# Gate/up product of a mixture-of-experts kernel with the weights as stationary operand, copied by ScalarE, in place of transposing the product's result

## The reference

```
x = x + attention(layernorm(x))              # 16 heads, 4 kv heads, window of 32
h = layernorm(x)                             # 8192 tokens
w, selected = sparsemixer(h @ router_w.T)    # two of 8 experts for each token
for e in range(8):
    g = silu(h @ w_gate[e].T) * (h @ w_up[e].T)      # 256 features
    out += dense_w[:, e:e+1] * (g @ w_down[e].T)
x = x + out
```

## Time and profile before

| | us |
|---|---|
| median of 3 runs | 601.63 |
| lowest, highest | 601.54, 603.01 |
| the profiled execution | 603.13 |
| its span, first to last instruction | 601.3 |
| PE, DVE, POOL, ACT busy in the span | 531.7, 446.0, 337.1, 332.9 |
| mean granted TensorE clock | 0.970 |

### The profile page before, as it was taken

One profiled execution on the slowest core, in us unless ns is written; L12 is line 12 of the kernel. 1 busy time (PEld: TensorE's weight loads), 2 busy tenths in 40 slices (PEclk: granted clock), 3 DMA queues, 4 the chain that ended last, 5 costly groups with the idle time before them and its releaser, 6 DMA issues. The chain is left out here.

```text
span 601.3 us, 20442 instructions
## 1 busy us (share of the span) xinstructions
PE 531.7 (88%) x6060; PEld 382.0 (64%) x6060; DVE 446.0 (74%) x1764; ACT 332.9 (55%) x1171; POOL 337.1 (56%) x468
## 2 busy tenths in 40 slices
PE   0599999899999999999984799999999999999970
PEld 0267787677777777777763466666666666666650
DVE  2569999999999999999999455646565555656553
ACT  1446776667767667767653455454544455444530
POOL 1222221866668766668754748264655655557655
PEclk9999999999999999999998599999999999999995
DMA  9512211332223322212231223244655554554543
GB/s 304 186 36 45 46 28 37 73 68 63 58 66 75 71 52 48 51 55 59 57 84 49 76 85 119 76 132 130 164 140 142 146 141 136 143 147 132 150 112 86
DMA packets 123530, 58.06 MB, mean 97 GB/s; under 512 B 53793, under 2 KB 118689, under 8 KB 123169
## 3 DMA queue, kind: packets, MB, share of 16 engines
q1 hardware_dynamic: 112640, 34.90, 23.6%
q0 software_dynamic: 8192, 16.79, 9.9%
q10 hardware_dynamic: 2592, 5.07, 2.2%
HBM read 28.14 MB, written 24.64 MB: 88 GB/s over the span
## 5 line engine op out<-in xcount | busy, mean ns | idle before, releaser
L1205 POOL DMA_INDIRECT expert_in<-xn,slot_r x128 | 127.5, 996 | 88.5 <-DVE slot_r L837 64.4
L1274 POOL DMA_INDIRECT ga<-expert_out,row_all x128 | 122.2, 954 | 92.4 <-DVE yb L1168 30.4
L653 PE MATMUL chb<-wgu,xbT 128*128 x288 | 151.1, 607 | 0.0
L1161 DVE TENSOR_TENSOR h<-sil,chb 128x256 f32<-128x256 f32 x144 | 60.6, 421 | 102.3 <-ACT sil L466 102.2
L381 ACT ACTIVATE pT<-chb 128x512 f32<-128x512 f32 x128 | 76.5, 598 | 83.6 <-DVE mx L854 49.2
L466 ACT ACTIVATE sil<-chb 128x256 f32<-128x256 f32 x144 | 55.4, 384 | 121.4 <-PE chb L653 121.4
L667 PEld LDWEIGHTS chb<-ident,h 128*128 128x128 f32 x288 | 40.5, 142 | 79.0 <-issue 42.5
L854 DVE TENSOR_REDUCE mx<-chb 128x8 f32<-128x512 f32 x128 | 85.4, 676 | 2.6 <-PE chb L577 2.1
L667 PE MATMUL chb<-ident,h 128*128 128x128 f32 x288 | 55.6, 275 | 1.5 <-DVE h L1161 1.4
L1229 POOL TENSOR_TENSOR tq<-t,rr 128x128 f32<-128x128 f32 x64 | 27.0, 421 | 48.7 <-issue 44.2
L596 PE MATMUL pp<-wp,xyT 128*128 128x272 f32 x128 | 50.2, 476 | 4.2 <-DVE t L939 2.6
(11 more groups left out here) (142 smaller groups left out, 1156.6 us busy)
## 6 DMA issues: line engine op xcount, KB each, us to landing
xb<-expert_in SPq DMA_DIRECT2D x144, 64.0 KB, 1.8
expert_out<-yb SPq DMA_DIRECT2D x72, 128.0 KB, 1.9
xa<-x SPq DMA_DIRECT2D x16, 256.0 KB, 3.1
out<-oo SPq DMA_DIRECT2D x32, 128.0 KB, 2.1
qk<-qk SPq DMA_DIRECT2D x64, 48.0 KB
wgu<-w_gu ACTq DMA_DIRECT2D x1, 2048.0 KB, 8.8
expert_in<-xn,slot_r POOLq DMA_INDIRECT x128
ga<-expert_out,row_all POOLq DMA_INDIRECT x128, 2.6
```

The costliest lines, as they stand in the source:

```text
L653: nc.tensor.matmul(chb[:, b % 2, :], xbT[:, b % 4, :], wgu[:, e, :], start=True, stop=True).then_inc(gu_done, 1)
L1161: nc.vector.tensor_tensor(h[:, b % 4, :], sil[:, b % 2, :], chb[:, b % 2, FF:2 * FF], ALU.mult).then_inc(h_ok, 1)
L1205: nc.gpsimd.indirect_dma_start(xs_dram, bass.IndirectOffsetOnAxis(ap=slot_r[:, q % 4, 2 * v + k:2 * v + k + 1], axis=0), xn2[:, t % 16, :] ...
L1274: nc.gpsimd.indirect_dma_start(ga[:, q % 2 * TPS + v, j, :], None, ys_dram[0:blocks * P, :], bass.IndirectOffsetOnAxis(ap=row_all[:, q * T ...
```

## The change

The product L653 is turned round: the weights become the stationary operand, in four pieces of 128 columns (two of gate, two of up), and xbT the moving one. The result then has the expert's features in partitions and tokens in columns, gate in the first half of a bank and up in the second. That is the layout the down product needs, and DVE writes hT itself. The stage B_HT goes, with PE's two transposes and ACT's copy of hT. Since the expert's number is only known in a register, ACT copies the expert's 512 gate and up columns to a fixed tile wcur (three buffers) in a stage of its own, B_COPY = 3, after the xbT copy of the slot; it reads the word and works out the expert itself, and waits that the product three blocks before has been done. chb is used in four banks instead of two and two. The down product stays at lag 7. PE needs the expert for that one only and reads its word at slot 5 of 8 instead of 3.

```diff
@@ -52,7 +52,7 @@
 (L_TY, L_XN2, L_TX2, L_RT, L_RANK, L_SCAT) = (14, 19, 20, 20, 23, 27)
 STEPS = NT + L_SCAT
 
-(B_LOAD, B_BT, B_GU, B_HT, B_DN, B_STORE) = (0, 3, 5, 6, 7, 8)
+(B_LOAD, B_COPY, B_BT, B_GU, B_DN, B_STORE) = (0, 3, 3, 5, 7, 8)
 C_FIRST = 5
 MEM = 8
 S_MOE = NT + L_PV
@@ -202,7 +202,8 @@
         summed = sb("summed", [1, NB // U])
 
         xb, xbT = sb("xb", [P, U, DIM]), sb("xbT", [P, 4, P])
-        sil, h, hT = sb("sil", [P, 2, FF]), sb("h", [P, 4, FF]), sb("hT", [P, 4, FF])
+        wcur = sb("wcur", [P, 3, 2 * FF])
+        sil, hT = sb("sil", [P, 2, FF]), sb("hT", [P, 4, FF])
         yb = sb("yb", [P, U, DIM])
         ga = sb("ga", [P, 8, 2, DIM])
         acc, oo = sb("acc", [P, 2, DIM]), sb("oo", [P, 4, DIM])
@@ -235,8 +236,8 @@
             "cols_ok", "colsT_done", "tabs_ok", "tail_ok", "tail_in"))
         xb_in = [sem(f"xb_in{n}") for n in range(U)]
         yb_out = [sem(f"yb_out{n}") for n in range(4)]
-        bt_done, xbT_ok, gu_done, sil_ok, h_ok = (sem(n) for n in ("bt_done", "xbT_ok", "gu_done", "sil_ok", "h_ok"))
-        ht_done, hT_ok, dn_done, yb_ok = sem("ht_done"), sem("hT_ok"), sem("dn_done"), sem("yb_ok")
+        bt_done, xbT_ok, wcur_ok, gu_done = sem("bt_done"), sem("xbT_ok"), sem("wcur_ok"), sem("gu_done")
+        sil_ok, hT_ok, dn_done, yb_ok = sem("sil_ok"), sem("hT_ok"), sem("dn_done"), sem("yb_ok")
         limits_ok, row_chain, comb_ok = sem("limits_ok"), sem("row_chain"), sem("comb_ok")
         gath = [sem(f"gathered{n}") for n in range(2 * TPS)]
         stored = [sem(f"stored{n}") for n in range(2)]
@@ -458,22 +459,31 @@
             for s in range(S_MOE):
                 step(s)
 
+            word = {}
+
             def slot(s):
                 b = block_at(s, B_GU)
                 if b is not None:
                     act.wait_ge(gu_done, b + 1)
-                    wait(act, h_ok, b - 1)
-                    nc.scalar.activation(sil[:, b % 2, :], chb[:, b % 2, 0:FF], ACT.Silu).then_inc(sil_ok, 1)
-                b = block_at(s, B_HT)
-                if b is not None:
-                    act.wait_ge(ht_done, b + 1)
-                    wait(act, dn_done, b - 3)
-                    nc.scalar.copy(hT[:, b % 4, :], chb[:, 2 + b % 2, 0:FF]).then_inc(hT_ok, 1)
+                    wait(act, hT_ok, b - 1)
+                    nc.scalar.activation(sil[:, b % 2, :], chb[:, b % 4, 0:FF], ACT.Silu).then_inc(sil_ok, 1)
                 b = block_at(s, B_BT)
                 if b is not None:
                     act.wait_ge(bt_done, b + 1)
                     wait(act, gu_done, b - 3)
                     nc.scalar.copy(xbT[:, b % 4, :], tp[:, 0:P]).then_inc(xbT_ok, 1)
+                b = block_at(s, B_COPY)
+                if b is not None:
+                    if b == 0:
+                        act.wait_ge(c_moe, 32)
+                        act.wait_ge(tabs_ok, 1)
+                    if b == NBA:
+                        act.wait_ge(tabs_ok, 2)
+                    if b % U == 0:
+                        word[b // U] = act.value_load(packed[0:1, b // U:b // U + 1], min_val=0, max_val=EXP ** U - 1)
+                    e = word[b // U] >> b % U * (EXP - 1).bit_length() & EXP - 1
+                    wait(act, gu_done, b - 2)
+                    nc.scalar.copy(wcur[:, b % 3, :], wgu[:, e, :]).then_inc(wcur_ok, 1)
 
             for s in range(NB + B_STORE):
                 d = drain_at(s)
@@ -647,26 +657,19 @@
             def slot(s):
                 b = block_at(s, B_GU)
                 if b is not None:
-                    e = expert(b)
                     pe.wait_ge(xbT_ok, b + 1)
-                    wait(pe, h_ok, b - 1)
-                    nc.tensor.matmul(chb[:, b % 2, :], xbT[:, b % 4, :], wgu[:, e, :],
-                                     start=True, stop=True).then_inc(gu_done, 1)
+                    pe.wait_ge(wcur_ok, b + 1)
+                    wait(pe, hT_ok, b - 3)
+                    for n in range(4):
+                        last = nc.tensor.matmul(chb[:, b % 4, n * P:(n + 1) * P], wcur[:, b % 3, n * P:(n + 1) * P],
+                                                xbT[:, b % 4, :], start=True, stop=True)
+                    last.then_inc(gu_done, 1)
                 if s == NBA:
                     pe.wait_ge(tabs_ok, 2)
-                if s == 3:
+                if s == 5:
                     pe.wait_ge(tabs_ok, 1)
-                if s % U == 3 and s < NB:
+                if s % U == 5 and s < NB:
                     word[s // U] = pe.value_load(packed[0:1, s // U:s // U + 1], min_val=0, max_val=EXP ** U - 1)
-
-                b = block_at(s, B_HT)
-                if b is not None:
-                    pe.wait_ge(h_ok, b + 1)
-                    wait(pe, hT_ok, b - 1)
-                    for k in range(2):
-                        last = nc.tensor.transpose(chb[:, 2 + b % 2, k * P:(k + 1) * P],
-                                                   h[:, b % 4, k * P:(k + 1) * P], ident[:, :])
-                    last.then_inc(ht_done, 1)
 
                 b = block_at(s, B_BT)
                 if b is not None:
@@ -1157,9 +1160,9 @@
                 b = block_at(s, B_GU)
                 if b is not None:
                     dve.wait_ge(sil_ok, b + 1)
-                    wait(dve, ht_done, b - 3)
-                    nc.vector.tensor_tensor(h[:, b % 4, :], sil[:, b % 2, :], chb[:, b % 2, FF:2 * FF],
-                                            ALU.mult).then_inc(h_ok, 1)
+                    wait(dve, dn_done, b - 3)
+                    nc.vector.tensor_tensor(hT[:, b % 4, :], sil[:, b % 2, :], chb[:, b % 4, FF:2 * FF],
+                                            ALU.mult).then_inc(hT_ok, 1)
 
                 b = block_at(s, B_DN)
                 if b is not None:
```

## The result

The changed kernel takes **584.39 us** at the median (583.86 to 585.49); the kernel before took 601.59 beside it. The ratio is 0.9717, 95% interval 0.9699 to 0.9734: faster by 17.2 us, where 24 to 26 were forecast and 577 was predicted. The profiled executions differ by 18.6 us in their spans (601.3 and 582.7).

The account below looks back on a forecast made before the run. PE, full in the expert part, was taken as the bound: 5.4 us by slot 36 plus 18.4 later moves POOL's last gathers 23.8, so 24 to 26, taken as 25, off about 602: 577 us. Range 571 to 589.

Parts of the forecast that it names:

- PE's slot: Expert part: one block's PE work falls from 1.635 to 1.443 us, 13 instructions of 0.111 us, 0.192 us less.
- rivals 3 and 4: Expert part: fresh-weight pairs at 0.135 us, about 602 us (0.04); loads not overlapping, 2.86 us a slot (0.01).
- Rival 3: Expert part: PE loses the gain through fresh-weight pairs of 0.135 us or a lower clock; about 602 us; chance 0.04.
- ACT's copy: Expert part: new copy 0.63 us long, 0.50 start to start; ACT 0.99 to 1.47 us per slot, 1.2 taken.
- Rivals 1 and 2: Expert part: ACT sets the pace, 588 us (0.13); the copy is much dearer, at 1.0 us 625 us (0.06).
- rival 1: Expert part: ACT sets the pace at 1.54 us per slot, gain 13.5 us, 588 us; chance 0.13.
- (a): Slots 3 to 14, router steps mixed in: PE reaches slot 14 about 1.0 us earlier (2.5 earlier to 1 later).
- The prediction's own warning: ACT's new order: the prediction is wrong if another stall like that at slot 12 comes; no size given.
- (b): Slots 14 to 35: 21 x 0.192 = 4.0 us gained, plus 0.4 from the gap at slot 24 going.
- (c): Slots 36 to 47: SP's tail clears set the pace, so nothing gained; the stretch just starts 5.4 us earlier.
- (d): Slots 47 to 143: 96 x 0.192 = 18.4 us gained.
- (e): The end: POOL's last 16 gathers bind and start 23.8 us earlier; up to 25.7 if the idle 1.95 us goes.

Follow-up runs that it names:

- a_copy2: Changed kernel with a second, unused 128 x 512 copy on ACT before each wcur copy; 592.23 us.
- after: The changed kernel itself, as profiled, without any follow-up edit; 584.39 us, ratio 0.9717 to the kernel before.
- b_copy: Kernel before with ACT's copy of an expert's columns, word and registers added but not used; 605.07 us, ratio 1.0051.
- b_notab: Kernel before without ACT's two table loads in slot 12, the last exponential replaced by input plus one; 601.31 us, ratio 0.9978.
- a_notab: Changed kernel without ACT's two table loads in slot 12, the last exponential replaced by input plus one; 583.07 us, ratio 0.9674.
- a_clears: Changed kernel with SP's eight tail clears in every fourth slot from 24 instead of one per slot from 36; 582.94 us, ratio 0.9692.
- a_nocopy: Changed kernel without ACT's copy, its word and registers, PE always reading expert 0's weights; 581.36 us, ratio 0.9659.
- a_tabs: Changed kernel with ACT's two table loads in slots 12 and 13 put between other instructions; 586.35 us, ratio 0.9735.

## Why the prediction was right or wrong

The sign and the mechanism were right, and 584.39 lies in the range. The value was 7 us too low: 17.2 us were gained of 25. By the profiles, against the steps of the prediction:

- **PE's slot.** Forecast 1.443 us, measured 1.449. The load/multiply pairs with fresh weights run at 0.111 us each, as L684 did; rivals 3 and 4 are ruled out. (Rival 3's sum was off: pairs of 0.135 us make a slot of 1.755, some 14 us slower and not equal; equality is at 0.126, as it says too.) The Trainium skill ("TensorE: Matmul & The Clock Gate", the section on packing small matmuls) has a list by which a weight load overlaps running matmuls only where their row groups differ; PE busy 129.99 us of 130 with 129.31 of loads beside it says that the loads, all of them 128 rows high, overlap in this kernel too. That section of the Trainium skill also names loads into a background weight buffer, which these rows would fit.
- **ACT's copy.** Forecast 0.63 us long (613 ns by the other estimate) and 0.50 from start to start, measured 0.629 and 0.52. Taken as 1.2 us of ACT per slot, measured 1.00: the register work is hidden except at word loads. The 0.35 us at the top of its sum stood on no row; ACT's register instructions of a copy take 0.04 to 0.05 us each, three of them in most slots. Rivals 1 and 2 are ruled out as rates, and a_copy2 shows rival 1's mechanism when ACT has really no room.
- **(a) Slots 3 to 14: failed.** Slot 14 was to come 1.0 us earlier; it came 0.66 earlier and slot 15 came 0.19 later, at the lower clock. Of this lead 0.56 us is chance: slot 0's load already came that much earlier. The step counted the new copies among the work of slots 3 to 11 but not as part of the stall that the table loads make, and it put half-clock slots only before slot 8; in after slot 8 (1.94 us) and slot 14 (2.58) ran partly at the lower clock too. b_copy shows 1.08 us for the copy there, and b_notab and a_notab that the loads cost 1.65 before and 4.0 after. Against the forecast 1.4 us are missing at slot 15, 2.0 without the chance lead. The prediction's own warning, a stall like that at slot 12, was the right place.
- **(b) Slots 14 to 35: right, with some luck.** From slot 15 to 36 the gain is 4.04 of 4.2. The 0.4 us at slot 24 came, and for the reason given: in after DVE's integer instruction is as long as before (1.77 us), and the product hT of the block begun at 371.86 starts at 374.55, 2.69 us later instead of about 1.5. It ends at 374.96, and the down product asks for it at 375.76, two slots on, where PE does not wait; before, the transposes asked one slot on. The step did not see that the 1.68 us are POOL's work beside DVE's. With the cast of eight numbers long as well (a_notab, a_clears, a_nocopy) 1.1 to 1.4 us are lost all the same, so the forecast was lucky in the cast's 0.27.
- **(c) Slots 36 to 47: right that nothing is gained, too high by 1.1.** The gain falls from 3.85 at slot 36 to 2.72 at slot 47. SP was taken to keep its pace; its rows of after hold two issues of 0.62 and 0.76 us where 0.34 to 0.43 is usual. From the first clear to the last SP took 16.84 us against 16.51 before, which is 0.3 of the 1.1; what makes the rest is open.
- **(d) Slots 47 to 143.** Forecast 18.4, measured 17.18: 96 x 0.006 = 0.6 is the slot of 1.449, the rest small gaps of PE (0.05 to 0.34 us) at word slots. a_nocopy, whose ACT reads no words, has 1.0 less in slots 48 to 143. The prediction had a word load fit in 0.8 us of slack, which it almost does.
- **(e) The end: failed by 1.6.** PE reaches slot 143 19.90 us earlier, but the last 16 gathers begin 18.33 earlier, at 556.71 against 575.04. What comes last there is new:

```profile
552.31 3.56 DMA expert_out<-yb
...
556.71 0.94 POOL ga L1277
557.66 1.95 issue
559.61 0.94 POOL ga L1277
```

Not a combine of DVE ends POOL's wait, as in the earlier trace rows, but the landing of the store issued in slot 143. It took 3.56 us; the same store, issued at 572.01 in the kernel before, landed after 1.86. All fourteen profiles agree: from slot 143's start to the first of these gathers it takes 3.5 us in the five without the change, where this store lands after 1.8 to 2.0 us, and 4.4 to 5.4 us in the nine with it, where it lands after 2.8 to 3.9; in eight of the nine POOL's wait ends with that landing. In after this is 0.8 of the 1.6 us: POOL began its last gather of the sequence before at 554.66 and, at its pitch of 1.25, could not have begun the next ahead of 555.91. Why the store lands later is open, and no experiment took it away. The 1.95 us idle comes again, as the choice of 24 to 26 allowed; what it is stays open, as no run removed it.

The gathers were to move by 23.8 us, to which I added 1.2, and moved by 18.3. Of these 6.7 us, 1.4 are missing by slot 15 (the table loads), 0.2 in slots 15 to 36, 1.1 in 36 to 47, 1.2 in the steady state, 1.6 at the store before the end, and 1.2 were my addition. Of the 18.6 us between the two profiled spans 0.56 are the earlier load of slot 0; the 18.0 left are within a microsecond of the 17.2 of the medians.

## What to carry to other kernels

A saving per slot on the engine that sets the pace is worth its rate only where that engine is full: list the stretches in which another queue sets the pace, and price the new instructions in each of those, since 0.63 us of copy was free in 130 slots and cost 0.7 us beside router steps and 1 to 2 us behind two table loads. A faster slot also eats the reserve of every other queue at once; here SP went from 84% to 95% of its fuller slot pairs (2.76 of 3.27 and of 2.90 us), and spread-out work that had cost nothing began to cost. Where a tiny instruction is long in a trace, look at what the neighbouring engines did in exactly that time before calling the instruction slow.

## What the runs showed of the hardware

- DVE's small cast and scalar instructions with integer output took 0.15 and 0.18 us alone, and up to 3.05 and 1.77 us beside a POOL TENSOR_TENSOR, ending with it. The cast of 3.05 us stood beside a POOL instruction of 3.48. It is not integers alone: in after the fp32 instruction L1177 (acc from ga, w and xa) took 1.17 us at 530.05, beside POOL's TENSOR_TENSOR of 529.78 (1.27 us), and 0.34 at 550.69, beside none. The product L1164, which reads one of its two operands from PSUM, took 0.41 to 0.42 us in all its 144 places.
- The granted clock fell after PE had idled 1.90 us in after, and after 2.42 in a_tabs. It did not fall after the same stall of 1.90 in a_clears (PE below: the next eight instructions take 1.06 as always), nor after 2.24 in b_copy. So in these four the length of the idle time alone doesn't decide, and what does is open.

```profile
353.38 0.30 PE L679 MATMUL tp<-ident,xb 128*128 128x128 f32 x1 [1.90 <-issue]
...
354.34 1.06 PE L664 MATMUL chb<-xbT,wcur 128*128 128x128 f32 x8
```

- The same DMA issue on SP's queue takes 0.34 to 0.43 us as a rule, and now and then 0.6 to 1.7. Landing took 3.46 and 3.56 us in the two places above, where the second one's store took 1.86 in the kernel before. Why is open.
